# Macaron blocks: the normed tile formed on ScalarE, and the product with V placed eight at a time in four PSUM banks

## What is computed

```
for i in range(DEPTH):                       # DEPTH = 6
    x = attn_layer(shift_tokens(x), Wqkv[i], q_scale[i], k_scale[i], Wo[i]) + x
    x = ffn_layer(shift_tokens(x), ln_g[i], ln_b[i], W1[i], b1[i], W2[i], b2[i]) + x

# attn_layer: 16 heads of 64; q and k are l2-normed, scaled and rotated; a query of a
# 32-token window sees its own window and the one before it
attn = softmax(einsum('bhwie,bhwje->bhwij', bq, bk2) * 8 + mask)
out  = einsum('bhwij,bhwje->bhwie', attn, bv2)        # the product with V
return out.reshape(b, n, INNER) @ Wo

# ffn_layer
xn = (x - mu) / sqrt(var + 1e-5) * g + bln            # the normed tile
```

## Time and profile before

| | us |
|---|---|
| median of three runs | 4460.64 |
| the profiled execution | 4477.24 |
| its span (first to last instruction) | 4475.5 |
| PE busy | 4041.9 (90%) |
| DVE busy | 3321.2 (74%) |
| POOL busy | 2698.0 (60%) |
| ACT busy | 2634.5 (59%) |
| mean granted clock of PE | 0.954 |

### The profile page before, as it was taken

One profiled execution on the slowest core, in us unless ns is written; L12 is line 12 of the kernel. 1 busy time (PEld: TensorE's weight loads), 2 busy tenths in 40 slices (PEclk: granted clock), 3 DMA queues, 4 the chain that ended last, 5 costly groups with the idle time before them and its releaser, 6 DMA issues.

```text
span 4475.5 us, 161417 instructions
## 1 busy us (share of the span) xinstructions
PE 4041.9 (90%) x70897; PEld 2574.2 (58%) x70897; DVE 3321.2 (74%) x5612; ACT 2634.5 (59%) x4548; POOL 2698.0 (60%) x3554
## 2 busy tenths in 40 slices
PE   5999999999999999589999999999999986899985
PEld 3666666666666666456666666666666654333333
DVE  6887777888878777478787888777788854566654
ACT  3666666666666666156666666666666642366651
POOL 5777777777777776387777777777777760000000
PEclk9999999999999999799999999999999997599996
DMA  2000000000000000000000000000000000000000
GB/s 82 5 5 24 9 22 7 9 24 5 9 24 9 24 5 9 21 3 10 7 21 9 24 5 10 24 9 24 4 9 5 5 4 0 0 1 1 1 1 9
DMA packets 75299, 53.51 MB, mean 12 GB/s; under 512 B 48472, under 2 KB 71400, under 8 KB 72944
## 3 DMA queue, kind: packets, MB, share of 16 engines
q1 hardware_dynamic: 74608, 43.28, 3.5%
HBM read 35.93 MB, written 1.05 MB: 8 GB/s over the span
## 4 chain that ended last, share of the span: by engine, by line
PE 66%; DVE 18%; issue 7%; ACT 4%; POOL 4%; DVEq 0%; SPq 0%; POOLq 0%; DMA 0%; ACTq 0%
PE psum L338 8%; PE psum L349 8%; PE psum L360 7%; PE psum L422 7%; DVE turn L626 6%; PE psum L385 5%; PE psum L403 5%; PE psum L414 3%; DVE den L671 3%; PE psum L1148 3%; PE psum L502 3%; PE psum L485 3%; PE psum L1117 2%; PE psum L492 2%; PE psum L1136 2%
## 5 line engine op out<-in xcount | busy, mean ns | idle before, releaser
L626 DVE TENSOR_TENSOR turn<-psum,ropes 128x512 f32<-128x512 f32 x1536 | 937.4, 671 | 25.2 <-POOL qkr L735 20.0
L742 POOL TENSOR_TENSOR turn<-turn 128x1024 f32<-128x1024 f32 x384 | 903.5, 2376 | 7.6 <-DVE turn L626 7.5
L338 PE MATMUL psum<-wqkv,xT 128*128 128x512 f32 x1536 | 766.7, 622 | 40.9 <-DVE turn L626 39.1
L521 ACT ACTIVATE sq<-psum 128x512 f32<-128x512 f32 x768 | 455.6, 593 | 573.9 <-PE psum L338 573.8
L735 POOL TENSOR_TENSOR qkr<-turn,rn 128x1024 f32<-128x1024 f32 x384 | 753.8, 1984 | 15.1
L769 POOL TENSOR_TENSOR scratch<-scratch,rden 128x1024 f32<-128x1024 f32 x192 | 365.3, 1903 | 656.2 <-DVE rden L674 656.2
L403 PEld LDWEIGHTS psum<-scratch,V 32*64 32x64 f32 x29952 | 547.4, 132 | 184.5 <-issue 182.9
L403 PE MATMUL psum<-scratch,V 32*64 32x64 f32 (+1 forms) x29952 | 593.0, 222 | 8.2 <-issue 6.5
L349 PE MATMUL psum<-wqkv,xT 128*64 128x512 f32 x1536 | 430.2, 639 | 127.1 <-DVE turn L626 126.9
L360 PEld LDWEIGHTS psum<-ident,qkr 128*128 128x128 f32 x3072 | 336.6, 144 | 350.9 <-ACT kT L530 153.7
L360 PE MATMUL psum<-ident,qkr 128*128 128x128 f32 x3072 | 474.9, 289 | 13.8 <-POOL qkr L735 13.8
(11 more groups left out here) (181 smaller groups left out, 6376.2 us busy)
## 6 DMA issues: line engine op xcount, KB each, us to landing
wqkv<-in_L_ffn_Wqkv_dram SPq DMA_DIRECT2D x12, 1536.0 KB, 7.3
wo<-in_L_ffn_Wo_dram SPq DMA_DIRECT2D x12, 512.0 KB, 7.4
zs<-Y SPq DMA_DIRECT2D x192, 31.8 KB
w<-in_L_ffn_W_dram SPq DMA_DIRECT2D x12, 341.0 KB
zs<-Y SPq DMA_DIRECT2D x168, 0.2 KB
w<-in_L_ffn_W_dram SPq DMA_DIRECT2D x12, 128.0 KB
rope<-in_shape_consts_dram SPq DMA_DIRECT2D x1, 1024.0 KB
X<-in_L_attn_x_dram SPq DMA_DIRECT2D x2, 512.0 KB
```

The lines of the kernel that those rows point to most:

```text
L338: pe.matmul(bank[b][:, :], xT[:, n // TPB % 2, bass.ts(n % TPB, P)], wqkv[n // TILES % 2][:, INNER * w:INNER * w + INNER].rearrange("p (h ...
L521: act.activation(sq[:, q // 2, q % 2, :, :], bank[QK_BANK[q]][:, :].rearrange("p (h d) -> p h d", d=RH), ACT.Square).then_inc(sem("squared ...
L626: e = dve.tensor_tensor(dst, src, tab.unsqueeze(1).broadcast_to([P, HEADS, RH]), ALU.mult)
L742: pool.tensor_tensor(t1, t1, turn2[:, w, :, :, :].rearrange("p a h d -> p (a h d)"), ALU.add).then_inc(sem("added"), 1)
```

## The change

Two things change in the macaron stage.

The normed tile moves from DVE to ACT. POOL forms `off` = -mean x rstd, one 128x1 `tensor_scalar`, after its Newton rounds; ACT forms `zn` = rstd x input + `off` with two `Identity` activations of 128x64 between `keep_qk(k, 0)` and the copies of `aT`. ACT waits for `unit_offset` before them, and DVE's `bn_aggr` waits for `unit_offset` in place of `unit_normed`.

`attend` uses eight places. For each block both column halves are used, so that the two heads of the same parity are side by side; outputs go to banks 0 and 1 for e = 0 and to banks 5 and 6 for e = 1, each row group having a bank of its own. Since banks 0 and 1 hold the scores, `attend(o, 0)` waits for `centred` of tile t, and `turn_p(t, 0)` waits for the first copy of `aT`. The rows of `Wo` are loaded in another order, with four DMAs in place of one (`AW` is 7 in place of 4).

```diff
@@ load_attention_weights
-            sp.dma_start(wo[i][:, :, :], W["Wo"][of, :, :].rearrange("(c p) f -> p c f", p=P)).then_inc(s, 16)
+            rows = W["Wo"][of, :, :].rearrange("(a r d) f -> r d a f", r=4, d=DH)
+            for e, c0, r in ((0, 0, 0), (0, 1, 2), (1, 0, 3), (1, 1, 1)):
+                sp.dma_start(wo[i][DH * c0:DH * c0 + DH, 4 * e:4 * e + 4, :], rows[r]).then_inc(s, 16)
@@
-        OUT_BANK, TURN_BANK, WO_BANK, MIX_BANK, UNIT_BANK = (5, 6), (7, 5, 6, 7), 5, 6, 7
+        OUT_BANK, TURN_BANK, WO_BANK, MIX_BANK, UNIT_BANK = ((0, 1), (5, 6)), (7, 5, 6, 7), 5, 6, 7
@@ attend
-                for i in range(4):
-                    for blk in range(-1, 4):
-                        for x in range(2):
-                            s = half ^ x
-                            if blk % 2 != s or (blk < 0 and starts_batch(n)):
-                                continue
-                            p = 4 * x + i
-                            q0, q1 = max(WIN * blk, 0), min(WIN * blk + NWIN, P)
-                            for e in range(2):
-                                r0 = DH * e + WIN * s
...
-                                mm = pe.matmul(bank[OUT_BANK[x]][DH * e:DH * e + DH, P * i + q0:P * i + q1],
+                for i in range(6):
+                    for x in range(2):
+                        s = half ^ x
+                        blks = [blk for blk in range(-1, 4) if blk % 2 == s and not (blk < 0 and starts_batch(n))]
+                        if i >= 2 * len(blks):
+                            continue
+                        blk = blks[i // 2]
+                        q0, q1 = max(WIN * blk, 0), min(WIN * blk + NWIN, P)
+                        v = V[(n if blk >= 0 else n - 1) % 3]
+                        for e in range(2):
+                            r0 = DH * e + WIN * s
+                            for c0 in range(2):
+                                p = 4 * x + 2 * (i % 2) + (c0 ^ e)
+                                o0 = P * (i % 2)
+                                mm = pe.matmul(bank[OUT_BANK[e][x]][DH * c0:DH * c0 + DH, o0 + q0:o0 + q1],
                                                v[r0:r0 + WIN, blk // 2 % 2, p, :], pT[r0:r0 + WIN, p, q0:q1],
-                                               start=first, stop=half == 1, skip_group_check=True)
+                                               start=(half == 0 and i == 0), stop=half == 1, skip_group_check=True)
@@ turn_p
+                    if on(n - 1):
+                        pe.wait_ge(sem("aT_kept"), part(n - 1, "aT_kept", 0))
@@ macaron_pe step
-                    for i in range(2):
-                        refill(OUT_BANK[i], ("aT_kept", part(o, "aT_kept", i)))
+                    for b in OUT_BANK[1]:
+                        refill(b, ("aT_kept", part(o, "aT_kept", 1)))
+                    if on(t):
+                        pe.wait_ge(sem("centred"), part(t, "centred"))
@@ macaron_act step
+                if on(z):
+                    act.wait_ge(sem("unit_offset"), part(z, "unit_offset"))
+                    if on(z - 1):
+                        act.wait_ge(sem("mixed"), mixed(s - 1))
+                    act.activation(zn[:, 0:HALF], Y[:, z % TILES, 0:HALF], ACT.Identity, bias=off[:, :],
+                                   scale=rn[:, 32:33])
+                    act.activation(zn[:, HALF:D], zs[:, z % 2, :], ACT.Identity, bias=off[:, :],
+                                   scale=rn[:, 32:33]).then_inc(sem("unit_normed"), 1)
...
-                        act.activation(aT[:, 4 * i:4 * i + 4, :], four(OUT_BANK[i]), ACT.Copy).then_inc(
-                            sem("aT_kept"), 1)
+                        b = OUT_BANK[i][0]
+                        act.activation(aT[:, 4 * i:4 * i + 4, :].rearrange("p (x i) q -> p x (i q)", x=2),
+                                       psum[:, b:b + 2, 0:2 * P], ACT.Copy).then_inc(sem("aT_kept"), 1)
@@ macaron_dve step
-                if on(z):
-                    dve.wait_ge(sem("rnorm"), at.step(s - 1))
-                    if on(z - 1):
-                        dve.wait_ge(sem("mixed"), mixed(s - 1))
-                    dve.tensor_scalar(zn[:, 0:HALF], Y[:, z % TILES, 0:HALF], mv[:, 0:1], rn[:, 32:33], ALU.subtract,
-                                      ALU.mult)
-                    dve.tensor_scalar(zn[:, HALF:D], zs[:, z % 2, :], mv[:, 0:1], rn[:, 32:33], ALU.subtract,
-                                      ALU.mult).then_inc(sem("unit_normed"), 1)
...
-                        dve.wait_ge(sem("unit_normed"), part(z, "unit_normed"))
+                        dve.wait_ge(sem("unit_offset"), part(z, "unit_offset"))
@@ macaron_pool step, after rsqrt(s)
+                if on(v):
+                    pool.wait_ge(sem("rnorm"), at.step(s))
+                    if on(v - 1):
+                        pool.wait_ge(sem("unit_normed"), part(v - 1, "unit_normed"))
+                    pool.tensor_scalar(off[:, :], mv[:, 0:1], rn[:, 32:33], -1.0, ALU.mult, ALU.mult).then_inc(
+                        sem("unit_offset"), 1)
```

More of the change, by code:

```diff
@@ L155, in build @@
         zn = sb("zn", [P, D])
+        off = sb("off", [P, 1])
         st6 = sb("st6", [P, 2, 6])
@@ L273, in build @@
         zero_row = const[1:2, 384 + 4 * TPB * DH:384 + 4 * TPB * DH + HALF]
-        AW = 4
+        AW = 7
         def load_attention_weights(sp, layer):
@@ L388, in attend @@
             def attend(n, half):
-                for i in range(4):
-                    for blk in range(-1, 4):
-                        for x in range(2):
-                            s = half ^ x
-                            if blk % 2 != s or (blk < 0 and starts_batch(n)):
-                                continue
-                            p = 4 * x + i
-                            q0, q1 = max(WIN * blk, 0), min(WIN * blk + NWIN, P)
-                            for e in range(2):
-                                r0 = DH * e + WIN * s
-                                v = V[(n if blk >= 0 else n - 1) % 3]
-                                first = half == 0 and i == 0 and blk == min(
-                                    k for k in range(-1, 4) if k % 2 == s and not (k < 0 and starts_batch(n)))
-                                mm = pe.matmul(bank[OUT_BANK[x]][DH * e:DH * e + DH, P * i + q0:P * i + q1],
+                for i in range(6):
[13 more added lines that the diff above has]
+                                mm = pe.matmul(bank[OUT_BANK[e][x]][DH * c0:DH * c0 + DH, o0 + q0:o0 + q1],
                                                v[r0:r0 + WIN, blk // 2 % 2, p, :], pT[r0:r0 + WIN, p, q0:q1],
-                                               start=first, stop=half == 1, skip_group_check=True)
+                                               start=(half == 0 and i == 0), stop=half == 1, skip_group_check=True)
                 mm.then_inc(sem("attended" if half else "half_attended"), 1)
@@ L691, in step @@
                     dve.wait_ge(sem("unit_var"), part(v, "unit_var"))
-                elif on(z):
+                if on(z):
                     dve.wait_ge(sem("unit_normed"), part(z, "unit_normed"))
@@ L760, in step @@
             def step(s):
-                u, k, t = s + 2, s + 1, s
+                u, k, t, v = s + 2, s + 1, s, s - 3
                 if on(k):
```

## The result

The changed kernel takes 4428.38 us, the median of 14 runs (4406.13 to 4457.40), against 4460.87 us (4440.37 to 4479.33) for the kernel before in the same comparison: a ratio of 0.993, 95% interval 0.9905 to 0.9955. It is faster by 0.7%, where 5% was forecast: 32 us in place of 222.

What follows compares the result with a forecast made beforehand. PE was taken to bound plain and out steps, DVE gate steps. Saving 4.2 us per group over 46 groups (193), plus 22 for early and 7 for rotary steps, made 222: 4255 profiled, scaled to 4239 us; range 4200 to 4320.

Steps and rivals of the forecast that it cites:

- The move of `zn`: Normed tile leaves DVE's chain: 0.50 us less in plain steps; without faster `attend`, gate steps fall 2.05 to 17.95.
- the first rival: `attend` doesn't speed up, column halves of one row group take turns; only DVE's part counts, 121 us, 4340; chance 0.12.
- DVE's chain as the next limit: Start of `project_v(k, 0)`: DVE ready at 8.12 us, PE at 7.70, so 0.42 us of PE's gain isn't paid out.
- The up step bound by the exponential's table: Up step: ACT reloads its table behind the gelu, so `project_v(k, 0)` stays at 9.13 us and the step at 18.22.
- ACT's two activations at no cost: Two 64-element activations after `keep_qk(k, 0)`: 0.4 us each, 0.8 for both, covered by 0.8 us before PE needs `aT`.
- The waiting for `centred`: Before `attend`: centring ends at 4.00 us, `attend` begins at 4.19, hidden; late by some 2 us only where rotary tables are scaled.
- The rule set against the eight places: Weight loads overlap matmuls only when the row group differs, so column halves queue and a half stays 1.51; given little weight.
- h: Time of a half of `attend`, 80 instructions: from 1.51 to 0.93 us, gaining 0.58 per half and 1.16 per step for PE.
- The gate step: From 20.00 to 17.3 us (-2.7); POOL's scaling half done 5.5 us in, PE's 0.42 slack absorbing all but 0.1.
- A new wait: Rival: a new wait on ACT or POOL decides, giving back 30 to 130 us, some 4300; chance 0.10.
- the clock's rival: Clock falls behind PE's 1.4 us waits in up steps; if all 46, 70 us come back, 4309; chance 0.08.
- The steps that scale the rotary tables: Ten out steps where DVE is the bound and `zn` goes: gain 1.4 us each in place of 0.74, 7 us in all.

Runs made afterwards that it cites:

- the second buffer: Changed kernel plus a second buffer for the q half of `turn1`, so `rotate(u, 0)` doesn't wait for POOL's scaling of the tile before: 4403.18 us, ratio 0.9877.
- the burst above: Kernel before, with score products issued ten times over on four tiles, 1280 pairs without a wait: 4589.53 us in one execution; ten-fold scores take 35 us.
- the halves apart: Changed kernel with `project_qk(u, 3)` moved between the two halves of `attend`: 4346.43 us, ratio 0.973.
- the table loaded early: Changed kernel with the halves apart, the second buffer and a one-column exponential on ACT right behind the gelus: 4253.66 us, ratio 0.9499.

## Why the prediction was wrong

**The terms that held.** The move of `zn`: -2.05 per gate step with four places, as the first rival's sum had it, measured 20.0 to 17.94. DVE's chain as the next limit at 8.12 us: measured 8.13. The up step bound by the exponential's table at 9.13: as said, and removing the load confirmed it. ACT's two activations at no cost: they take 0.43 us each, and PE waits for them only where the pipeline fills and drains. The waiting for `centred`, hidden in ordinary steps: held. The rule set against the eight places, by which a half would stay at 1.51, did not come true: halves take 1.07.

**h was mis-sized**, 1.07 for 0.93, and by itself it cost nothing, since DVE was the limit (the second half takes 1.04, and PE's path would be 8.86 - 0.44 - 0.47 = 7.95).

**The gate step, the smaller of the two steps that failed.** The prediction placed POOL's first L745 at 5.5 us into the step and asked only what PE does with it. It left out that `rotate(u, 0)` writes the buffer that this operation reads, and so waits for it too; the centring and statistics end at 4.2. Before, the wait for POOL inside `zn` covered this one. This is 1.2 us in each gate step behind a plain step of the forecast length, shown by the second buffer (18.50 to 17.24, and 47 us once the gaps were rare). Where a stall goes, one has to say what is late next; that was done for PE and not for DVE.

**The supply of instructions, the larger one.** The prediction put it at nothing without a word. The term of `attend` took the rate of the scores, 11.6 ns a pair, as a property of eight places. That rate holds for one dense stretch of 128 pairs, and the burst above shows that some 250 pairs can run before the supply counts; the prediction didn't ask whether it holds for three stretches in seven microseconds. The changed kernel asks for 128 + 6 + 80 + 4 + 80 pairs in 7 us, where 256 instructions take 3.7 us to come. Its gaps are 84 us by themselves; the 63 steps with a gap and with group work are together 106 us longer than their forecast lengths, the lapses of the clock behind the gaps included. None of the rivals had this. "A new wait" (0.10) named ACT and POOL alone; the clock's rival (0.08) had the lapses, but behind waits in up steps, and 70 us of them.

**The clock.** The forecast let the lapses move or vanish at no cost. Measured, 39 of the changed kernel's 190 steps have a stretch of the lower granted clock, 27 of them steps with a gap, against 15 steps before; the mean granted clock went from 0.954 to 0.940. With the halves apart it is 0.954 again.

**The steps that scale the rotary tables** were to gain 1.4 us each, from 20.77 where nothing disturbs them. Two of the ten do, at 19.36; with the normed tile alone all ten take that. The other eight take 20.5 to 25.8, and the ten on average as long as before. The new wait for `centred` is 1.9 us in eight of them, as forecast, and the prediction gave it no price, since DVE is the bound there. But in seven of the ten a stretch of the lower clock lies in the step with this wait, and with the halves apart and the second buffer, again in seven, such steps take 20.6 to 20.8 us. In two of the changed kernel's steps the scaling also meets POOL's pair as described above, and the wait grows to 3.9 and 5.4 us.

In sum, of the 169 us between the forecast for the profiled execution (4255) and its time (4424), the gaps with their lapses hold some 106, the 24 gate steps without a gap 19 and the steps with the rotary tables 25. Up to 8 more are a slip of the sum, which reckoned with 46 groups where the trace has 44 gate steps between one L385 and the next. The rest lies in the early steps and in lapses without a gap; I did not split it further. These were reckoned from one execution. The causal part rests on the runs: with the gaps made rare and the buffer's wait removed, the forecast's own undisturbed steps come back (17.3, 18.22, 17.32 and 14.64), with 4299 us; with the table loaded early as well 4254. That kernel is still 60 us over the forecast of 4239; it has 23 gaps, and 17 of its steps have a stretch of the lower clock. That 4254 is near 4239 says nothing for the forecast, since the early load is a third edit that it didn't have.

## What to carry to other kernels

Two changes that each look local can share a hidden resource: here the normed tile alone gave 3.0%, `attend` alone cost 2.5%, and together they gave 0.7%; moving two matmuls made it 2.7%. When small products are packed more densely, count the instructions per microsecond over the whole stretch and not per product; gaps ended by nothing in the profile, at even distances in the count of instructions, are the sign. And before a wait is removed, list every engine that waits for the same buffer behind it.

## What the runs showed of the hardware

PE's instruction stream of this kernel is refilled 256 instructions at a time, one block in 3.7 us in a long dense stretch (14.5 ns per instruction), of which the packet of 16384 bytes takes 0.9 to 1.4 us; about 500 instructions run before the first gap. A stretch that issues a pair in 11.6 to 13.4 ns, as the scores and the halves of `attend` do, outruns the 29 ns a pair of the supply by more than twice. Each of the 70 gaps ends 1.20 to 1.60 us after such a packet.

A longer wait can cost more than its own length. In the kernel with eight places alone, PE waits 3.1 us for DVE in most gate steps without a gap, against 1.9 before, and matmuls at the lower clock follow; gate steps were 1.3 us longer on average than before, those with gaps included, though PE had less to do.

Two DVE operations that read two SBUF tensors took 1.81 and 2.13 us in place of 0.41 when a pair of POOL's 128x1024 operations had begun before them.
